# Output projection before the query projection in a round, and router rows turned by DMA transfers

## What is computed

```python
x = x + cross_attention(layernorm(x), ctx, ctx, w_q, b_q, w_k, b_k, w_v, b_v, w_o, b_o)   # 16 heads of 16, 77 keys
x = x + ffn(layernorm(x), router_w, gate_w, up_w, down_w)                                   # 8 experts, F = 1024

def ffn(x, ...):
    probs = softmax(x @ router_w)
    top_w, top_i = top_k(probs, 2)
    cw = zeros.at[token, top_i].set(top_w)
    for e in range(8):
        h = silu(x @ gate_w[e]) * (x @ up_w[e])
        out = out + cw[:, e:e + 1] * (h @ down_w[e])
```

## The kernel before

| stage | engine | what it does |
|---|---|---|
| `turn_x`, `turn_att` | TensorE | transpose the normalized input of a (L647), the attention output of c (L732) |
| `project_q`, `project_o` | TensorE | 12 matmuls for the queries of a, 14 for the output of c (two of them the bias, L744) |
| `split_x`, `split_att`, `split_q` | ScalarE | high parts xt_hi (L925), at_hi (L950), q_hi (L932) |
| `low_x`, `low_att`, `low_q` | VectorE | low parts xt_lo (L1155), at_lo (L1218), q_lo (L1184) |
| `residual` | VectorE | x2 = x + attention output, out of PSUM (L1227) |
| `normalize`, `sum_x`, `gather` | VectorE | divide by the softmax sum (L1209, L1213), statistics (L1132), gathering them for the layernorm (L1144) |
| `turn_x2`, `copy_x2`, `router` | TensorE, ScalarE, TensorE | transpose the normalized rows of r in fp16 (L755), copy them out of PSUM (L955), logits of 8 experts |

## Time and profile before

### The profile page before, as it was taken

One profiled execution on the slowest core, in us unless ns is written; L12 is line 12 of the kernel. 1 busy time (PEld: TensorE's weight loads), 2 busy tenths in 40 slices (PEclk: granted clock), 3 DMA queues, 4 the chain that ended last, 5 costly groups with the idle time before them and its releaser, 6 DMA issues.

```text
span 908.5 us, 32045 instructions
## 1 busy us (share of the span) xinstructions
PE 843.3 (93%) x11936; PEld 770.9 (85%) x11936; DVE 588.6 (65%) x1757; ACT 479.8 (53%) x900; POOL 342.4 (38%) x637
## 2 busy tenths in 40 slices
PE   4889899899999987799999999999999999999995
PEld 3677777777777776699999999999999999999995
DVE  6789788788888756566466457446646648544442
ACT  5777777788887774444354335324424435333331
POOL 4789566655666555241122221222222122222112
PEclk9999999999999989899999999999999999999999
DMA  6211322222222543495355228225525632223221
GB/s 211 88 46 45 95 76 66 80 79 68 84 82 66 110 147 119 93 201 132 50 99 122 29 55 174 36 39 108 118 30 99 135 60 36 35 29 32 35 35 18
DMA packets 109876, 74.04 MB, mean 81 GB/s; under 512 B 66444, under 2 KB 99802, under 8 KB 109818
## 3 DMA queue, kind: packets, MB, share of 16 engines
q1 hardware_dynamic: 83898, 36.09, 16.9%
q0 software_dynamic: 13536, 19.85, 12.3%
q10 hardware_dynamic: 12384, 17.35, 7.5%
HBM read 36.27 MB, written 26.80 MB: 69 GB/s over the span
## 4 chain that ended last, share of the span: by engine, by line
PE 75%; issue 5%; ACT 4%; DVE 4%; POOL 1%; DMA 1%; another core or an unknown queue 1%; ACTq 0%; SPq 0%; DVEq 0%; POOLq 0%
PE bank L630 16%; PE bank L632 16%; PE bank L631 16%; PE bank L825 6%; PE bank L827 6%; PE bank L826 6%; PE bank L699 3%; PE bank L706 3%; ACT probs L938 1%; ACT pt_hi L944 1%; DMA raw_tail<-expert_rows 1%; DVE xt_lo L1155 1%; PE bank L755 1%; ACT xt_hi L925 1%
## 5 line engine op out<-in xcount | busy, mean ns | idle before, releaser
L630 PE MATMUL bank<-xg,e_hi 128*128 128x128 f16 x2176 | 374.6, 220 | 5.2 <-issue 3.4
L632 PE MATMUL bank<-xg,e_lo 128*128 128x128 f16 x2176 | 374.6, 220 | 0.5 <-issue 0.5
L631 PE MATMUL bank<-xg,e_hi 128*128 128x128 f16 x2176 | 374.6, 220 | 0.0
L1702 POOL DMA_INDIRECT out<-y_sb,tok_row x67 | 108.4, 1618 | 425.8 <-DVE y_sb L1456 404.2
L630 PEld LDWEIGHTS bank<-xg,e_hi 128*128 128x128 f16 x2176 | 214.0, 98 | 7.2 <-issue 3.1
L631 PEld LDWEIGHTS bank<-xg,e_hi 128*128 128x128 f16 x2176 | 214.0, 98 | 2.8 <-issue 1.2
L632 PEld LDWEIGHTS bank<-xg,e_lo 128*128 128x128 f16 x2176 | 214.0, 98 | 0.0
L1008 ACT ACTIVATE g_act<-bank 128x512 f32<-128x512 f32 x136 | 81.2, 597 | 223.0 <-PE bank L632 207.1
L1461 DVE SCALAR_TENSOR_TENSOR h_full<-bank,g_act 128x512 f32<-128x512 f32 x136 | 94.0, 691 | 121.7 <-ACT g_act L1008 120.7
L825 PE MATMUL bank<-e_hi,h_hi 128*128 128x256 f16 x544 | 148.9, 274 | 4.5 <-DVE h_lo L1467 3.1
L827 PE MATMUL bank<-e_hi,h_lo 128*128 128x256 f16 x544 | 148.8, 274 | 0.9 <-issue 0.8
(11 more groups left out here) (193 smaller groups left out, 1685.8 us busy)
## 6 DMA issues: line engine op xcount, KB each, us to landing
e_stage<-in_gate_w ACTq DMA_DIRECT2D x24, 256.0 KB
e_stage<-in_up_w ACTq DMA_DIRECT2D x22, 256.0 KB
e_stage<-in_down_w ACTq DMA_DIRECT2D x20, 256.0 KB
expert_rows<-pads SPq DMA_DIRECT2D x8, 530.0 KB
xin<-in_x SPq DMA_DIRECT2D x16, 256.0 KB, 3.0
xres<-in_x SPq DMA_DIRECT2D x16, 256.0 KB
out<-x SPq DMA_DIRECT2D x16, 256.0 KB
k_diag<-k_parts SPq DMA_DIRECT2D x124, 9.6 KB
```

The costliest lines, as they stand in the source:

```text
L630: pe.matmul(dst, a_hi(c), b_hi(c), start=c == 0, stop=False)
L631: pe.matmul(dst, a_hi(c), b_lo(c), start=False, stop=False)
L632: mm = pe.matmul(dst, a_lo(c), b_hi(c), start=False, stop=ends and c == chunks - 1)
L1702: pool.indirect_dma_start(out, bass.IndirectOffsetOnAxis(tok_from[:], 0), y_from[:], None, compute_op=ALU.add).then_inc(added, 16)
```

## The change

Four things move in the tables, and one stage goes to another engine.

- TensorE: `turn_att` stands ahead of `turn_x` in step 1; `project_o` is in step 2 and `project_q` in step 3; the router is in step 6, at its end, instead of step 5.
- ScalarE: `split_att` stands ahead of `split_x` in step 1; `split_q` goes from step 3 to the end of step 4.
- VectorE: `low_att` goes to step 2 inner, `low_x` to step 2 outer, `residual` from outer 4 to outer 3, `low_q` from outer 4 to inner 5, that is, between the maximum and the shift of unit 6; `route_top` starts behind the shift of step 7 instead of ahead of its maximum.
- The rows of r are turned by two transposing DMAs of SyncE per batch, one for each half of the tokens, straight from `rows` to `x2t` in SBUF. They wait for the rows and for the router before, and stand behind `spread_keys` and ahead of the store and the load. `turn_x2` on TensorE and `copy_x2` on ScalarE are left for batches 14 and 15, in `last_rounds`. `x2t` has its parts in another order for that.

```diff
--- before.py
+++ after.py
...
@@ -388,6 +389,10 @@
             return bool(b) and not early_pieces(n)
+        def by_pe(r):
+
+            return r.reg is None and r.plus >= B - 2
+
         def is_first(j):
             return bool(j) and j.reg is None and j.plus == 0
@@ -534,9 +539,20 @@
                 for h in heads:
                     spread_key(sp, j.plus % 2, h)
-            def round_of(j):
+            def turn_x2(r):
+
+                after(sp, row_ready, r.value(2, 2))
+                after(sp, logits_made, r.value(1))
+                apart(sp, passed)
+                for t in range(NT):
+                    sp.dma_start_transpose(x2t[:, :, t * P:(t + 1) * P],
+                                           rows[:, rows_at(r), t, 0:D].bitcast(F16)).then_inc(x2_landed, 16)
+
+            def round_of(j, r=None):
                 load_a(j)
                 spread_keys(j - 1)
+                if r:
+                    turn_x2(r)
                 store_c(j - 3)
                 load_c(j - 2)
@@ -551,7 +567,7 @@
             round_of(At(3))
             with sp.Fori(0, (B - 4) // 2) as k:
                 for odd in range(2):
-                    round_of(At(4 + odd, k, 2))
+                    round_of(At(4 + odd, k, 2), At(odd, k, 2))
             def load_second(chunks):
                 for n in chunks:
@@ -564,13 +580,16 @@
                 load_tile(sp, slice(g * TILE, (g + 1) * TILE))
             spread_keys(At(B - 1))
+            turn_x2(At(B - 4))
             sp.wait_ge(e_lo_ready, PIECES)
             load_second(range(0, 3))
             landed(sp, At(HELD_FROM))
             load_rows(0)
             store_c(At(B - 3))
             load_c(At(B - 2))
-            load_second(range(3, 7))
+            load_second(range(3, 5))
+            turn_x2(At(B - 3))
+            load_second(range(5, 7))
             store_c(At(B - 2))
             load_c(At(B - 1))
             load_second(range(7, 9))
@@ -752,17 +771,21 @@
                 for c in range(KC):
                     for l in range(2):
                         for t in range(NT):
-                            mm = pe.transpose(ps_x2t[:, c, l, t * P:(t + 1) * P],
+                            mm = pe.transpose(ps_x2t[:, l * KC + c, t * P:(t + 1) * P],
                                               parts[:, t, l * D + c * P:l * D + (c + 1) * P], ident16[:])
                 mm.then_inc(x2_turned, 1)
             def router(r):
-                after(pe, x2t_ready, r.value(1, 1))
+                if by_pe(r):
+                    pe.wait_ge(x2t_ready, r.plus - (B - 3))
+                else:
+                    after(pe, x2_landed, r.value(16 * NT, 16 * NT))
+                    after(pe, slots_ready, r.value(1))
                 first_use(r, w_lo_ready, 5)
                 for t in range(NT):
                     mm = three(ps_logits[:, t, :],
-                               lambda c: x2t[:, c, 0, t * P:(t + 1) * P], lambda c: x2t[:, c, 1, t * P:(t + 1) * P],
+                               lambda c: x2t[:, c, t * P:(t + 1) * P], lambda c: x2t[:, KC + c, t * P:(t + 1) * P],
                                lambda c: r_hi[:, c, :], lambda c: r_lo[:, c, :], KC)
                 mm.then_inc(logits_made, 1)
@@ -780,11 +803,10 @@
             def body(n, a, b, c, r, z):
                 extra = {0: [(z, ranks)],
-                         1: [(not is_first(a) and a, turn_x), (c, turn_att)],
-                         2: [(a, project_q)],
-                         3: [(c, project_o)],
-                         4: [(r, lambda r: turn_x2(r, rows_at(r)))],
-                         5: [(r, router)],
+                         1: [(c, turn_att), (not is_first(a) and a, turn_x)],
+                         2: [(c, project_o)],
+                         3: [(a, project_q)],
+                         6: [(r, router)],
                          7: [(n, project_k), (is_first(n) and n, turn_x), (n, project_v)]}
                 for u in range(UNITS):
                     if at := unit(c, b, a, u + 2):
@@ -951,8 +973,9 @@
             def copy_x2(r):
-                after(act, x2_turned, r.value(1, 1))
-                act.activation(x2t[:].rearrange("p c l s -> p (c l s)"), ps_x2t[:].rearrange("p c l s -> p (c l s)"),
+                act.wait_ge(x2_turned, r.plus - (B - 3))
+                act.wait_ge(logits_made, r.plus)
+                act.activation(x2t[:].rearrange("p n s -> p (n s)"), ps_x2t[:].rearrange("p n s -> p (n s)"),
                                ACT.Copy).then_inc(x2t_ready, 1)
             def split_weights(e, parity, n):
@@ -985,11 +1008,11 @@
                 second = a and a.reg is None and a.plus == 1
                 extra = {0: [(a and not second, lambda _: norm(a, 0, xin, xn, xt_turned, 1, xn_ready, m)),
                              (first, lambda _: split_x(a)), (first, lambda _: spread_half())],
-                         1: [(not first and a, split_x), (c, split_att)],
+                         1: [(c, split_att), (not first and a, split_x)],
                          2: [(r, lambda j: norm(j, 1, x2, x2n, row_ready, 2, x2n_ready, m))],
-                         3: [(a, lambda j: split_q(j, j.plus % 2)), (first, lambda _: split_later()), (first, lambda _: clear_keys(1)),
+                         3: [(first, lambda _: split_q(a, a.plus % 2)), (first, lambda _: split_later()), (first, lambda _: clear_keys(1)),
                              (first, lambda _: norm(n, 0, xin, xn, xt_turned, 1, xn_ready, n))],
-                         4: [(r, copy_x2)],
+                         4: [(not first and a, lambda j: split_q(j, j.plus % 2))],
                          7: [(r, router_exp)]}
                 for u in range(UNITS):
                     if (at := unit(c, b, a, u - 1)) and at[1] in LOW_ON_ACT:
@@ -1349,20 +1372,21 @@
                 slots_chain = take_slots(z, z.plus % 2) if z else None
-                inner = {2: [(a, low_x)],
+                inner = {2: [(c, low_att)],
+                         5: [(a, lambda j: low_q(j, j.plus % 2))],
                          3: [(n, lambda j: sum_x(j, 0, xin, x_in, 16, x_summed)),
                              (r, lambda j: high_rows(j, rows_at(j)))]}
                 outer = {0: [(a, full_kv)],
                          1: [(c, lambda j: normalize(j, 1))],
-                         2: [(c, low_att)],
-                         4: [(c, residual), (a, lambda j: low_q(j, j.plus % 2))],
+                         2: [(a, low_x)],
+                         3: [(c, residual)],
                          5: [(b, lambda j: normalize(j, 0)), (c, lambda j: sum_x(j, 1, x2, x2_ready, 1, x2_summed)),
                              (m, lambda j: gather(j, n, c) if by_pool(n, b) else start(statistics(j, n, c)))],
-                         6: [(z, lambda j: finish(weights_chain)), (z, lambda j: finish(slots_chain))]}
+                         6: [(z, lambda j: finish(weights_chain)), (z, lambda j: finish(slots_chain))],
+                         7: [(r, lambda j: start(route_top(j)))]}
                 starts = {1: [(z, lambda j: start(weights_chain))],
-                          2: [(z, lambda j: start(slots_chain))],
-                          7: [(r, lambda j: start(route_top(j)))]}
+                          2: [(z, lambda j: start(slots_chain))]}
                 for u in range(UNITS):
                     for at, stage in starts.get(u, []):
                         if at:
```

5 lines of the change are left out of this document (3 added, 2 removed).

## The result

The changed kernel takes 948.71 us in the median of 4 runs (946.07 to 952.47), the kernel before 917.04 (916.41 to 921.15): a ratio of 1.033, with an interval of 1.029 to 1.037. It is slower, as forecast, but by about 32 us and not by 20, and 2.7 us above the upper end of the range. The profiled execution took 950.45 us, with a span of 948.7 and a mean granted clock of 0.945 instead of 0.985. That last number was not in the forecast.

The account below looks back on a forecast made before the run. Bound taken: a ring of short operations between engines, plus a second across rounds through gather and scatter. 910.35 us profiled + 15 x 1.35 = 20.3 gives 930.6; the 6.7 us difference to the median gives 937.3, range 916 to 946.

Parts of the forecast that it names:

- the place named: On VectorE between the maximum and shift of unit 6: the low part of the queries waits for ScalarE, 1.8 us or more.
- The high bound 1.75 (the whole delay of VectorE): Most a round was said to grow, 1.75 us: the full delay of unit 6's shift on VectorE; 26.3 us over 15 rounds.
- The term of 1.35 us: Growth per round over ScalarE and TensorE, from the later exponential of unit 7; 15 rounds give 20.3 us.
- So a later gather makes a later next round: Second ring across rounds: VectorE's statistics gather releases GpSimd's steps, then the scatter, to which the next step 1 copy seemed tied.
- The distance of 2.85 to 2.93 us: From the first scatter DMA's issue to ScalarE's step 1 copy; two equal distances were read as tying the copy to the scatter.
- The path over GpSimd: Gather, GpSimd's steps, scatter and release of the next round come 1.5 us later, after 0.27 us of slack.
- Part 2: Rows turned by SyncE's transfers instead of TensorE transposes and ScalarE's copy; removal and transfers were both costed at nothing.
- the rival "faster": VectorE's wait is filled and TensorE's freed 0.45 us per round comes through: 6.3 us gained, 910.7 us; chance 11%.
- The swap alone costs nothing on TensorE: Output and query projections change places at no cost, if the attention output is transposed as early as the input was.
- the bound from below that was taken (3.0): Landing time taken for the second transfer, from a plain load, at no cost; the rival with 8.1 us had 8%.
- The estimate of 10.5 us for the eight tiles: By the skill page's figure, SyncE's transposed tiles arrive 10.5 us after 227.2, costing 49 us over 14 rounds.
- The wait of turn_att: In step 1 on TensorE, waiting for the last normalized output: covered up to 0.87 us by the copy's remote wait.

## Why the prediction was right, and where it was wrong

*The direction and the mechanism were right.* VectorE waits in 15 rounds, in the place named, for 2.2 us (forecast: 1.8 or more), and shift, gather and exponentials move nearly as worked out. With the clock held up by useless matmuls the kernel takes 937.75 us; the forecast was 937.3. That these two agree so closely is luck, since two misses have opposite signs: a round at full clock grew by 1.76 us and not by 1.35, and the transfers gave something back that was put at nothing.

*The step that failed is the bound of the sum.* "The high bound 1.75 (the whole delay of VectorE)" took the longest delay of a link as the most that a round can grow. The cost of the clock stood at nothing, without a reason: TensorE, which VectorE's wait leaves nearly idle for some one and a half microseconds, works at half clock for some 7 us behind that in most of the rounds. With 1.76 us at full clock and about 3 us in rounds in which the clock falls, the true range per round was outside the one given. The earlier trace rows showed a clock of 1.00 with TensorE busy 22.46 of 25 us, and the prediction used it only to say that TensorE was not the bound. The Trainium skill, page "TensorE: Matmul & The Clock Gate", section "Part 1: The HAM clock gate (the "warmup" mystery)", says that the array runs at one of two clocks, by how busy it has been. The trace agrees: in the round shown 1.00 falls to 0.50, and to no other level, behind a stretch with little work. It should have been a rival here, since the change makes TensorE wait longer.

*The term of 1.35 us* was short by 0.4. Some 0.14 came in by ScalarE's copy of the queries, later than the place it was put in; the rest lies between the exponential of unit 7 (1.49) and the next round (1.76). The unseen wait of 1.08 us stands there, but no run separates its share.

*"So a later gather makes a later next round"* was wrong. The distance of 2.85 to 2.93 us was real, and was read as a chain from two rows. A later gather made the round shorter, and so did a later scatter. The path over GpSimd gave 1.5, close to what came, for a wrong reason.

*Part 2, costed at nothing,* was worth some 0.6% by itself (ratio 0.994), that is, 4 to 6 us. That is removal, transfers and later router together. In steady rounds the profile shows 19.30 to 19.53 us instead of 19.5, so no more than 1 to 2 us of that; where the rest comes from stays open. The 6.3 us of the rival "faster" are near it, but not for its reason, 0.45 us in each round, which the rounds do not show.

*"The swap alone costs nothing on TensorE"* held beside the late queries (ratio 1.033 with all of the new order, 1.029 with the late queries alone, intervals that overlap), but not without them: with transfers in all of them, the new order without the late split gave 1.010, or 1.006 with the input transposed first, and the old order 0.994. The unseen waits are the likely reason; it is not settled.

*The transfers* landed in time in all rounds of the changed kernel but one, and in a steady round within 3.4 us of the second issue, near the bound from below that was taken (3.0) and far from 8.1. The estimate of 10.5 us for the eight tiles, worked out from the 1309 ns that the Trainium skill, page "VectorE: DVE Perf Modes", section "The three transpose paths", gives for one tile, does not hold here: in the kernel with transfers alone the router ran 4.6 us after the first issue without waiting.

*The wait of turn_att* was covered in the changed kernel, as said (ratio 1.032 with the input first, 1.033 without). With VectorE's wait gone it stood on TensorE, 1.59 us in the round shown, but the unseen wait was behind it.

## What to carry to other kernels

When an operation moves to another place in an engine's order, look first at what its input's producer does at that time: here the producer's copy was moved one step later than the consumer could bear, and one entry moved back gave two thirds of the loss back. When a change makes TensorE wait, count the clock besides the wait, by rows of the same kernel at both levels. And a constant distance between two events is not a chain: move one of them and look whether the other follows.

## What the runs showed of the hardware

Two things had not been expected. Work that nobody needs can make a kernel faster: 168 matmuls kept TensorE's clock at 1.00 in ten of the fifteen rounds and saved about 11 us, and twelve additions on GpSimd, which moved a scatter by 1.15 us, took 0.9 us off the round shown. And behind the issue of an indirect DMA by GpSimd, other engines can see a result of TensorE late: a wait that the profile calls "remote" ended 2.1 to 3.0 us after the first scatter of a pair in the attention phase of the kernel before, of the runs with the query split back (VectorE and ScalarE, up to 1.91 us of waiting) and of the run with four additions. The step 1 copy of the round shown had no such wait where the scatter was issued as the transposes ended (twelve additions). The delay does not come behind every scatter, as the pair at 229.13 shows, and what else it takes stays open.
